# Sparse experts: a ring of sixteen gathered tiles instead of eight, and the experts' numbers loaded by TensorE in one place

## What is computed

```python
def _L1_ffn_ref(x, Wg, bg, W1, b1, W2, b2):
    gates = (jnp.einsum('bsd,de->bse', x, Wg) + bg) / (TEMP + 1e-06)
    weights, indices = jax.lax.top_k(gates, TOP_K)          # TOP_K = 2
    weights = jax.nn.softmax(weights, axis=-1)
    h = jax.nn.silu(jnp.einsum('bsd,edf->bsef', x, W1) + b1)
    all_out = jnp.einsum('bsef,efd->bsed', h, W2) + b2
    gathered = jnp.take_along_axis(all_out, indices[..., None], axis=2)
    return jnp.sum(gathered * weights[..., None], axis=2)
...
x = x + _L1_ffn_ref(_layernorm(x, axis=-1), L1_ffn_Wg, ...)
```

## Time and profile before

| | us |
|---|---|
| median of 3 runs | 997.29 |
| lowest, highest | 996.39, 999.38 |
| the profiled execution | 997.57 |
| its span (first to last instruction) | 995.2 |
| the loop: start of the first gather to start of the last scatter | 278.37 to 384.25 |

### The profile page before, as it was taken

The page is one execution under the profiler, slowest core; times in us unless marked ns, Lnnn a source line. Parts: engine busy times, 40 slices in busy tenths (PEclk is TensorE's granted clock), DMA queues, the critical chain, the costliest instruction groups (busy, mean ns, idle before and its releaser), DMA issues. The chain is left out here.

```text
span 995.2 us, 28553 instructions
## 1 busy us (share of the span) xinstructions
PE 838.3 (84%) x11485; PEld 630.4 (63%) x11485; DVE 728.3 (73%) x1701; ACT 572.3 (58%) x1319; POOL 439.8 (44%) x289
## 2 busy tenths in 40 slices
PE   2676997798469996789878999999999998968888
PEld 1556455686347676344556878878787876834567
DVE  4798776788745544788786859586776859889974
ACT  3471534567335553577686484756748483347774
POOL 3111212985057774487205353333526254529710
PEclk9697999999779997999978999999999999999999
DMA  7330000300511123000100101000000100000001
GB/s 221 87 125 1 1 1 25 153 2 2 213 52 53 53 51 107 1 1 2 51 4 2 29 3 28 3 29 4 29 23 8 29 3 3 3 1 1 2 2 43
DMA packets 26990, 36.16 MB, mean 36 GB/s; under 512 B 7563, under 2 KB 20300, under 8 KB 26094
## 3 DMA queue, kind: packets, MB, share of 16 engines
q1 hardware_dynamic: 21166, 27.92, 8.9%
q0 software_dynamic: 2496, 5.12, 1.9%
q10 hardware_dynamic: 3200, 1.31, 0.5%
HBM read 27.06 MB, written 7.27 MB: 35 GB/s over the span
## 5 line engine op out<-in xcount | busy, mean ns | idle before, releaser
L2178 DVE TENSOR_TENSOR soft_outs<-soft_expert_ps,soft_bias 128x512 f32<-128x512 f32 x128 | 87.3, 689 | 77.1 <-PE soft_expert_ps L1896 75.3
L1896 PE MATMUL soft_expert_ps<-soft_W,soft_slots 128*32 128x128 f32 x4096 | 126.3, 276 | 2.4 <-DVE soft_outs L2178 2.4
L1896 PEld LDWEIGHTS soft_expert_ps<-soft_W,soft_slots 128*32 128x32 f32 x4096 | 109.7, 111 | 21.5 <-issue 21.3
L1002 POOL TENSOR_TENSOR l_prob<-l_prob,l_inv 128x1024 f32<-128x1024 f32 x48 | 91.3, 1902 | 39.8 <-DVE l_inv L1156 39.4
L1988 ACT ACTIVATE soft_slots<-soft_slot_ps 128x512 f32<-128x512 f32 x128 | 69.4, 598 | 65.1 <-PE soft_slot_ps L1882 65.1
L2073 POOL TENSOR_TENSOR l_ring<-l_ring,soft_inv 128x1024 f32<-128x1024 f32 x15 | 35.1, 2370 | 103.5 <-DVE soft_inv L2171 54.6
L1141 DVE TENSOR_REDUCE l_under<-l_score 128x16 f32<-128x1024 f32 x48 | 58.6, 1222 | 27.1 <-PE l_score L1222 13.2
L1843 PE MATMUL soft_slot_ps<-phi,xnT 128*128 128x256 f32 x256 | 69.5, 409 | 7.8 <-ACT soft_spread L1976 4.7
L1105 ACT ACTIVATE l_probT<-l_turned 128x512 f32<-128x512 f32 x96 | 52.2, 594 | 33.8 <-PE l_turned L1031 33.8
L1031 PE MATMUL l_turned<-ident,l_prob 128*128 128x128 f32 x384 | 53.5, 283 | 21.0 <-POOL l_prob L1002 21.0
L1910 PE MATMUL soft_mix_ps<-soft_outs,soft_combT 128*32 128x128 f32 x2048 | 67.8, 273 | 2.1 <-DVE soft_acc L2194 2.1
(11 more groups left out here) (462 smaller groups left out, 2155.6 us busy)
## 6 DMA issues: line engine op xcount, KB each, us to landing
moe_w<-in_moe_W SPq DMA_DIRECT2D x2, 2048.0 KB, 10.0
soft_W<-in_soft_W SPq DMA_DIRECT2D x16, 256.0 KB, 2.8
kept<-early SPq DMA_DIRECT2D x1, 2048.0 KB, 6.3
l_keys<-in_moe_b SPq DMA_DIRECT2D x1, 2048.0 KB, 8.5
l_asked<-kept SPq DMA_DIRECT2D x1, 2048.0 KB, 13.3
ctxT<-in_ctxT SPq DMA_DIRECT2D x1, 1024.0 KB, 5.5
moe_rows<-xn_tok SPq DMA_DIRECT2D x4, 256.0 KB, 3.6
expert_rings<-moe_back SPq DMA_DIRECT2D x4, 256.0 KB, 5.5
```

The lines of the kernel that those rows point to most:

```text
L1002: nc.gpsimd.tensor_tensor(prob[t % 4][:], prob[t % 4][:], inv[t % 2][:].unsqueeze(2).broadcast_to(S16), ALU.mult).then_inc(share_done, 1)
L1896: last = nc.tensor.matmul(expert_ps[c][32 * j:32 * j + 32, h, tt, :], slots[u % 3][:, h, tt, 128 * c + 32 * j:128 * c + 32 * j + 32], W[i ...
L2178: nc.vector.tensor_tensor(outs[u % 3][:, c].rearrange("p h t d -> p (h t) d"), expert_ps[c][:].rearrange("p h t d -> p (h t) d"), bias[i % ...
```

## The change

The buffer xn has 16 parts of 128 columns; the gathered tiles now use all 16 (`ROWS` = 16) instead of the first 8. POOL issues gathers 0 to 15 ahead of scatter(0), and then scatter(0), gather(16), scatter(1), gather(17) and so on. `gather(i)` waits for the turn of tile i-16. The semaphores `gathered` are 16 instead of 8. The ring `given` of the finished tiles and its semaphores `scattered` stay at 8. PE loads the numbers of all tiles in three loads (15, 12 and 12) in a row ahead of the loop; those in steps 5 and 10 are gone. The counts of all instructions stay the same.

```diff
-    there, RING = lambda i: 0 <= i < TILES, 8
+    there, RING, ROWS = lambda i: 0 <= i < TILES, 8, 16
...
-        taken = [xn[:, r, :] for r in range(RING)]
+        taken = [xn[:, r, :] for r in range(ROWS)]
...
             def gather(i):
-                if i >= RING:
-                    pool.wait_ge(takenT_made, i - RING + 1)
-                nc.gpsimd.indirect_dma_start(taken[i % RING], None, rows_dram, bass.IndirectOffsetOnAxis(source[:, i:i + 1], 0)).then_inc(gathered[i % RING], 16)
+                if i >= ROWS:
+                    pool.wait_ge(takenT_made, i - ROWS + 1)
+                nc.gpsimd.indirect_dma_start(taken[i % ROWS], None, rows_dram, bass.IndirectOffsetOnAxis(source[:, i:i + 1], 0)).then_inc(gathered[i % ROWS], 16)
...
-            for i in range(RING):
+            for i in range(ROWS):
                 gather(i)
             for i in range(TILES):
                 scatter(i)
-                if there(i + RING):
-                    gather(i + RING)
+                if there(i + ROWS):
+                    gather(i + ROWS)
...
             def turn_taken(i):
-                pe.wait_ge(gathered[i % RING], 16 * (i // RING + 1))
+                pe.wait_ge(gathered[i % ROWS], 16 * (i // ROWS + 1))
                 if i >= 2:
                     pe.wait_ge(takenT_done, i - 1)
-                nc.tensor.transpose(moved[i % 2][:, 0:128], taken[i % RING], core.ident[:]).then_inc(takenT_made, 1)
+                nc.tensor.transpose(moved[i % 2][:, 0:128], taken[i % ROWS], core.ident[:]).then_inc(takenT_made, 1)
...
             pe.wait_ge(expert_done, 1)
-            learn(15)
+            for number in (15, 12, 12):
+                learn(number)
             pe.wait_ge(index_done, 2)
             turn_taken(0)
             for i in range(TILES + 3):
-                if i in (5, 10):
-                    learn(12)
...
-        core.gathered = [life.enter_context(nc.semaphore(f"gathered{r}")) for r in range(8)]
+        core.gathered = [life.enter_context(nc.semaphore(f"gathered{r}")) for r in range(16)]
```

## The result

The changed kernel takes 990.28 us (median of 5 runs, 987.63 to 991.97), the kernel before 997.54 (5 runs): a ratio of 0.992, 95% interval 0.9899 to 0.9941. The forecast was 990.0 us. The profiled executions, spans of 995.2 and 988.0 us, are 7.2 us apart. In them the loop, from the start of the first gather to the start of the last scatter, went from 105.88 to 100.20 us.

What follows compares the result with a forecast made beforehand. The prediction took POOL's gathers and scatters to bound the loop; issuing sixteen gathers ahead gains 7.26 us, so the profiled 997.57 becomes 990.3, or 990.0 us against the median of 997.29. The range was 988.7 to 992.5 us.

Steps and rivals of the forecast that it cites:

- The bound: In the loop, POOL sets the pace at 2.566 us a tile; its idle time at both ends is 7.2 us.
- the sum: Start of the last scatter: 376.99 instead of 384.25, a gain of 7.26 us if nothing else is late.
- POOL's queue: Ahead of scatter(0), POOL issues sixteen gathers in a row, 1.25 us each.
- The rival on the other side: Ahead of the loop's scatters, POOL's queue doesn't take sixteen gathers: 1000.0 us, slower than before; 4 in 100.
- The ring of results: In the loop, eight results suffice: margin 7.9 us at give(8), about 2.0 at give(30); DVE waiting then costs nothing.
- The price of the loads: Ahead of the loop, two loads of 12 take 2.9 us and fit into the 3.2 in which PE waits.
- I take the low one: At PE's start, 1.45 us for a load of 12, the low bound, instead of the trace's 2.914.
- The stall in step 5: In the loop, the load of numbers stalls PE 1.25 us; the remainder of its 2.9 lies behind matmuls.
- The prediction's own sign against it: At PE's start, the forecast would be wrong if the two added loads cost over 2 us each.
- PE sets the end: Rival at the loop's end: loads of 2.914 us make PE up to 2.7 late; gain 5.7, 991.6 us; 15 in 100.
- Behind the loop: From last scatter to PE's first addition, 6.67 us moves along unchanged; nothing later with its own time was found.
- The memset: Rival at the last scatters: DVE's memset of 3.47 us holds them up; gain 3.8, 993.5 us; 3 in 100.

Runs made afterwards that it cites:

- the kernel with the loop of 98.4 us: The changed kernel with loads of 16, 16 and 7 numbers instead of 15, 12 and 12; median 990.54 us, ratio to before 0.9929 to 0.9956.
- the changed one: The changed kernel, unaltered, timed once more; median 988.55 us (4 runs), ratio to the kernel before 0.9897 to 0.9937.

## Why the prediction was right, and where it was not

**The bound: right.** POOL set the pace, and its idle time of 7.2 us was what could be won. With loads that start at multiples of 16 bytes the loop is 105.88 - 98.41 = 7.5 us shorter, where the sum said 7.26; the difference is in the last scatters, 1.27 us apart instead of 1.29.

**POOL's queue: right.** Sixteen gathers at 1.25 us, the sixteenth at 296.80, 18.98 us after the first (19.00 forecast). The rival on the other side, a queue that doesn't take them, would have shown in the gaps and doesn't. The ring of results at eight never held TensorE back.

**The price of the loads: wrong.** This is the step that failed: "I take the low one." I had worked out 1.45 us for a load of twelve, from VectorE's loads of one number and TensorE's of fifteen, and had explained away the 2.914 us that the trace had for the very same instruction, as time behind matmuls. They took 2.87. The stall in step 5 was shorter (1.25 us) for another reason than I gave: the load began at 290.6 while TensorE's matmuls ran on until 292.6 (1.08 us before the turn at 293.65), so a part of its 2.9 us was covered. At the start of the loop nothing covers it beyond the 3.2 us in which TensorE waits for the first gather. Interpolating between 1 and 15 numbers took the length for what sets the price, and it is the byte at which a load starts. The prediction's own sign against it, loads that cost over 2 us each, is what the profile then showed.

**So the rival came true.** "PE sets the end", 15 in 100: gain 5.7 us in the loop, scatters that wait for `give` at the end. Measured 5.68, with the waits at 0.72, 1.22, 0.37 and 0.71 us.

**Behind the loop: right where I looked, and not the whole.** From the last scatter to the first addition it took 384.65 - 378.02 = 6.63 us, against 6.67. The memset cost nothing, where it lay in the changed kernel and where it lay inside the scatters. But the prediction took everything further on as fixed. In the two profiles, 0.55 us of the 7.20 come from ahead of the loop, 0.48 from between the last scatter and the sixth layer, and 0.49 from there to the end: no instruction there was changed, and the table shows that this last part differs by up to 3.9 us between profiles, by 3.4 between two executions of one program.

That the time of 990.28 us is only 0.3 from the forecast is thus luck, a sum of two errors: the loop gained 1.6 us less than forecast, and in the two profiles 1.5 us came from stages that the change doesn't touch. The rival's own 991.6 was also inside the range. What stays open is how the difference of the medians splits up. Loop lengths alone don't order the medians: the kernel with the loop of 98.4 us was timed at 990.54 beside the changed one's 988.55, with a loop of 100.0. No version was shown to beat the changed kernel.

## What to carry to other kernels

When an engine in a chain issues gathers and scatters and is itself the bound, count its idle time, not its busy time: gathers that don't depend on results belong ahead of the first wait, as many as it takes to reach the first result (twelve did here, eight didn't). When a trace has the duration of the very instruction that you move, take it at its full length, and ask what covered it where it stood. And a gain of a few microseconds in a long kernel can be as large as what the stages behind it differ by from one execution to the next; compare the stage's own length in two traces before you believe a total.

## What the runs showed of the hardware that I had not expected

- The load of numbers into TensorE's registers: 12 numbers in 0.86 to 1.04 us from a byte that is a multiple of 16, and in 2.87 us from bytes 60 and 108; 14 in 1.53 us from byte 0 and 3.36 from byte 56.
- The same program, executed again with an arrival 1.3 us later, took 3.4 us less for the remainder (501.8 and 498.5), with TensorE's granted clock at 1.00 instead of 0.87 in one stretch of 10 us. From the last scatter on, the difference is 1.6 us. 2.5 us of added work left the span of the profiled execution as it was (987.8 and 988.0), but that was the fastest of four.
